# GpSimd waits for the group two in front before it issues a group of gathers, from layer 1 on

## The reference

```python
for l in range(5):
    msg = norm[:, None] * (h[row] + edge_fea)
    agg = segment_sum(msg, col, num_segments=n)
    h = relu(concat([h, agg], axis=1) @ mlp_w[l] + mlp_b[l])
    h = batch_norm(h)            # and relu, but for the last layer
# then: shared expert + two routed experts of eight for each node, added to x
```

## Time and profile before

| | us |
|---|---|
| median of 3 runs | 6880.44 |
| lowest and highest of them | 6827.38, 6889.59 |
| the profiled execution, its own time | 6810.47 |
| span of its instructions | 6808.8 |
| layers 1 to 4 in it (1918 to 5460) | 3542 |

### The profile page before, as it was taken

The page is one execution under the profiler, slowest core; times in us unless marked ns, Lnnn a source line. Parts: engine busy times, 40 slices in busy tenths (PEclk is TensorE's granted clock), DMA queues, the critical chain, the costliest instruction groups (busy, mean ns, idle before and its releaser), DMA issues. The chain is left out here.

```text
span 6808.8 us, 114607 instructions
## 1 busy us (share of the span) xinstructions
PE 5077.8 (75%) x28957; PEld 3394.9 (50%) x28958; DVE 2045.5 (30%) x4409; ACT 1070.7 (16%) x2670; POOL 3252.0 (48%) x3312
## 2 busy tenths in 40 slices
PE   1333377777778878688887788876887869999998
PEld 0222355555544444444444444444444448888876
DVE  7734433333432222322224222232222252000012
ACT  1523300000120000200002000021000032222221
POOL 2888854444455555455554555545555505000014
PEclk9985588988889989898898898988898989999998
DMA  7045144444455555555555555545555531111113
GB/s 264 0 68 158 37 135 135 139 131 127 112 172 167 160 153 163 150 161 160 151 163 147 160 159 164 155 134 172 159 160 154 154 96 69 45 57 59 49 48 92
DMA packets 448168, 874.86 MB, mean 128 GB/s; under 512 B 115986, under 2 KB 261272, under 8 KB 445002
## 3 DMA queue, kind: packets, MB, share of 16 engines
q0 software_dynamic: 184544, 526.38, 27.8%
q10 hardware_dynamic: 97068, 178.12, 9.1%
q1 hardware_dynamic: 166334, 167.82, 8.1%
HBM read 725.48 MB, written 146.57 MB: 128 GB/s over the span
## 5 line engine op out<-in xcount | busy, mean ns | idle before, releaser
L1246 POOL DMA_INDIRECT sets<-rows,index x2480 | 2353.3, 949 | 1974.9 <-issue 714.4
L1938 PE MATMUL bank<-resid,arena 128*128 128x512 bf16 x4116 | 1461.8, 398 | 81.1 <-issue 78.0
L1939 PE MATMUL bank<-sets,arena 128*128 128x256 bf16 x4116 | 1163.2, 283 | 54.2 <-issue 53.4
L1867 PE MATMUL bank<-sets,row_out 128*128 x2432 | 893.8, 403 | 337.3 <-issue 271.4
L1868 PE MATMUL bank<-sets,row_out 128*128 x2432 | 697.7, 287 | 115.7 <-issue 114.2
L1938 PEld LDWEIGHTS bank<-resid,arena 128*128 128x128 bf16 x4116 | 419.4, 102 | 631.9 <-issue 232.9
L2277 PE MATMUL bank<-sets,arena 128*128 128x256 f32 x2480 | 630.2, 387 | 53.5 <-issue 22.5
L461 POOL DMA_INDIRECT dense<-sets x399 | 511.2, 1281 | 224.0 <-issue 106.2
L1276 ACT ACTIVATE index<-arena x620 | 127.3, 205 | 3050.6 <-issue 1605.5
L1867 PEld LDWEIGHTS bank<-sets,row_out 128*128 x2432 | 245.1, 101 | 657.3 <-issue 453.0
L2277 PEld LDWEIGHTS bank<-sets,arena 128*128 128x128 f32 x2480 | 479.3, 194 | 129.8 <-issue 27.4
(11 more groups left out here) (400 smaller groups left out, 5781.8 us busy)
## 6 DMA issues: line engine op xcount, KB each, us to landing
arena<-dense ACTq DMA_DIRECT2D x315, 384.0 KB
arena<-dense ACTq DMA_DIRECT2D x105, 416.0 KB
sets<-rows,index POOLq DMA_INDIRECT x2480
dense<-arena SPq DMA_DIRECT2D x21, 1568.0 KB, 20.9
expert_in<-zero SPq DMA_DIRECT2D x14, 1024.0 KB
expert_out<-zero SPq DMA_DIRECT2D x14, 1024.0 KB
rows<-resid SPq DMA_DIRECT2D x36, 384.0 KB, 2.7
arena<-expert_in SPq DMA_DIRECT2D x54, 256.0 KB, 2.7
```

Of the source, the lines that this page charges most:

```text
L1246: pool.indirect_dma_start(got0_words[:, j, 0:W0 // 2] if first else got[:, j, :], None, rows0 if first else rows, bass.IndirectOffsetOnAxi ...
L1867: pe.matmul(to[:, 0:2 * D], ones, rows_here[:, a:a + 2 * D], start=start, stop=False)
L1938: pe.matmul(bank[:, 5, 0:2 * D], cells, high_parts[:, s, :], start=t == 0, stop=False)
L1939: mm = pe.matmul(bank[:, 5, D:2 * D], cells, low_parts[:, s, :], start=False, stop=False)
```

## The change

In layers 1 to 4 GpSimd makes one more wait before it issues group g: `landed >= g + 3`. As the counter starts at 4, this says that SP has seen g-1 groups, that is, groups 0 to g-2, with their rows in SBUF and their one-hots made. `gated` adds one to a counter that nothing waits for. Layer 0 and everything behind the layers stay as they are, and so do the number of instructions on all other engines, all transfers and their sizes.

```diff
                             if not first:
                                 pool.wait_ge(group_done, now * R + (r + 1))
                                 gated(pool)
+                                pool.wait_ge(landed, now * R + (r + 3))
+                                gated(pool)
                             for j in range(r * K, r * K + K):
                                 pool.indirect_dma_start(
```

## The result

The changed kernel takes 6974.13 us (median, 6954.97 to 7004.72) against 6854.84 us of the kernel before beside it (6827.38 to 6889.59): a ratio of 1.0187, 95% interval 1.0141 to 1.0232. That is 119 us more; forecast were 49. The time lies inside the range of 6840 to 7040, and it is slower by over 1%, to which the prediction had given 0.35, less than the 0.50 of "within 1%".

What follows compares the result with a forecast made beforehand. PE was taken to set the pace, busy 2810 of 3542 us in layers 1 to 4 but not always fed. Stalls of 39 us plus 10 for the clock, 49, added to the median 6880.4 gave 6930 us, range 6840 to 7040.

Steps and rivals of the forecast that it cites:

- Who is held: GpSimd before its gathers: late one-hots of g-2 hold 169 of 488 groups, 609 us together.
- Rows never late: Gathers in layers 1 to 4: rows of g-2 land in time, so waiting for landing alone delays nothing.
- The stalls, 39 us: PE in layers 1 to 4: 25 or so stalls from late groups, most under 2 us, taken as 39 us.
- The worked case, group 179: PE at group 179: issue held to about 2285.6, usable at 2293.1, wanted at 2291.17, 1.9 us of stall.
- The mark of the prediction: Sign of being right: PE's waits at L1867 for L1187 grow from 64.8 us by some 40.
- The clock, 10 us: PE's granted clock: added idle costs 19 us at most, none if the clock is low already; taken as 10.
- Slow stepping, 0 with +20 on one side: PE's long steps without a wait, 163 us in layers 1 to 4: unchanged, or an eighth more, +20 us.
- The dense loads, 0: Dense loads behind ACT's indices: at least 10.9 us from issue to use covers the delay, so no cost.
- third mark: Sign of being wrong: dense matmuls (L1938) begin to wait; none waited for a DMA in the profile before.
- (1) Covered: Rival: all delays vanish in PE's lead, 0 to 15 us, 6885 us; chance 0.20.
- (2) Lockstep: Rival: DVE, gathers and PE hand stalls on; a fourth of 609 us reaches PE, 172 us, 7050; chance 0.22.
- (3) The gentler pace pays: Rival: GpSimd's pauses cut slow steps and late dense loads, -104 us, 6776 us; chance 0.18.

Runs made afterwards that it cites:

- landing only: Kernel before plus a GpSimd wait for the rows of group g-2 alone, not its one-hots: 6893.36 us, 1.0021 of the kernel before.
- the pair with a pause: Kernel before and changed kernel, each with a 0.92 us GpSimd memset behind every group's four gathers: 6769.41 us (0.9872) and 6855.25 us (0.9986).
- Short rows: Kernel before with gathers from layer 1 on fetching 512 bytes a row instead of 1536, sums wrong: 6798.19 us, 1.0041.
- the profiled pair: One profiled execution each of the kernel before (6810 us) and the changed kernel (6959.48 us).
- paused pairs: Kernel before with a 0.52 us GpSimd memset behind every second gather: 6695.89 us, 0.9852; in the last four runs 6043.16 us, 1.0566.
- the paced pair with it: With slow stepping: kernel before and changed kernel, each with a 0.92 us memset behind every group, 6769.41 and 6855.25 us.
- the paced pair without: Without slow stepping: kernel before and changed kernel, each with a 0.52 us memset behind every second gather, 6043.16 and 6036.13 us.
- double pause: Kernel before with two 0.92 us GpSimd memsets behind every group: 6901.05 us, 1.0174.
- the last runs: Four kernels with pauses of several forms, one also with the wait, under a condition where the kernel before took 5692.34 us: 5891.41 to 6155.82 us.

## Why the prediction was right or wrong

**Who is held.** Right. 170 groups were issued before `landed` of g-2 in the trace of before (169 by one-hots in the prediction), none after. The 0.8 us from one-hots to issue stands too: 109 groups are issued 0.8 to 0.9 us after `landed` of g-2. "About 170 cases" ended by L1187 were 134 in the view of waits. Their 637.7 us are GpSimd's whole idle time before them and not the delay that was worked out as 609, so that the two are alike proves nothing.

**Rows never late.** Right: landing only 1.0021 (0.9986 to 1.0057).

**The stalls, 39 us.** The mechanism was right, the term too small: PE's idle time before late groups rose from 34 to 109 us, by 75 (62 against landing only, 70 in the pair with a pause). Directly before held groups stand some 57 us; 14 of these stalls come at four places of the layer (groups 38, 55, 90 and 106 of 124), about 4 us each. In number the forecast was good, 25 or so stalls against 28 late groups more; their size was not. It had most of them under 2 us, 1.7 on average for the 43 us, and measured is 2.7. The worked case, group 179, is one: 3.69 us measured, 1.9 forecast, issue 0.9 us after the one-hots. The other 18 us or so are groups that follow a held one. The mark of the prediction, waits at L1867 for L1187 growing by 40, was badly chosen: that row went from 64.8 to 75.6 us only, because the profile puts most of these stalls under "issue", as it does the 3.69 us above.

**The clock, 10 us.** The term that was off by the largest factor, four to five. The excess of short steps went from 179 to 228 us: 49, and 40 against landing only, 40 in the pair with a pause. The bound of 19 us was made of the ratio of the time at half clock to the idle time. What it missed: the change makes 28 more late groups (10 before, 38 after), each an idle stretch of some us on PE, and with them the stretches at the lower clock rise from 79 to 125, from 683 to 843 us together. An average share per us of idle can't tell which idle brings the clock down; that it is these stretches is suggested by the two counts, not shown. Landing only speaks for caution: with little more idle time before late groups than before (47 us against 34) it has 97 such stretches, 799 us, and still an excess of only 188 us. What the change adds is lower clock while matmuls run.

**Slow stepping, 0 with +20 on one side.** Undersized from the start. I had counted the 296 steps of 0.7 us, 163 us; all steps over 0.6 us, those of 1.4 and 2.1 us in the earlier trace rows included, are 457 us in the same trace. An eighth more of that is 57, not 20. What the change adds to it isn't settled: 128 us against the profiled execution of before, 37 against landing only, -39 in the pair with a pause. One trace of each kernel can't tell. Wrong too was that gathers at place nine or later of a run rise from 256 to 392: with steps of under 1.4 us taken as one run, there are 265 in the trace of before and 228 in that of after.

**The dense loads, 0.** Nearly right: waits for them grew from 25 to 33 us. The prediction's third mark (dense matmuls begin to wait) was met by name, 131 to 242 us in front of them, but these "issue" waits were slow stepping, not loads. For the same reason the rule of the Trainium skill weighed there, "DMA: Bandwidth & Descriptors", section "Issuing engines are not separate DMA queues", gave nothing: its 131 us were no cost of shared DMA engines in this kernel. Short rows halved the traffic and gained nothing.

**The sum.** With the measured terms, 75 for the stalls, 49 for the clock, 8 for dense loads less 34 of turns and 60 of other waits (these two partly the same time, waited for elsewhere), and 128 of slow steps, it is 166 on the profiled pair; against landing only 62 + 40 + 9 + 37 - 68 + 11 = 91. The medians say 119, between the two. The forecast of 49 had the mechanism, but 119 lies outside its own 20 to 90 us, and 6974 just above its 6900 to 6970. That the time lies within 6840 to 7040 is owed to the room left there for lockstep. And by luck 6930 looks nearer to 6974 than it is: the 49 us were added to 6880, where the kernel before took 6855 beside the changed one.

**The rivals.** (1) Covered: refuted where slow stepping is, by 1.0187 and the pair with a pause. Without slow stepping, at least with paced gathers, the wait costs nothing that can be measured, but there hardly a group is held, so that nothing has to be covered. (2) Lockstep: its sum, 172 us, is close to the 169 of the profiled pair, but not by its mechanism: of the 609 us of holding 62 to 75 reach PE as late groups, about a tenth, not a quarter. Its mark, layer 1 over 865 us, was passed at 885, and told little: landing only, which costs next to nothing, took 852 there and 863 and 864 in layers 2 and 4. (3) The gentler pace pays: not with this wait. But the pace itself does where slow stepping is: pauses that are blind to DVE gained 1.3 and 1.5%.

**What lay under it.** The prediction took the late one-hots as the kernel's own rhythm. The paused pairs speak for another account: one-hots are late because PE, and with it DVE's `take`, falls behind in slow stepping. 67 groups of that kernel are issued before `landed` of g-2 with it, 2 without. So the change's price hangs on a condition of the machine: 1.3% in the paced pair with it, 0.1% (-0.4 to 0.6) in the paced pair without. The two pairs have pauses of another form (0.92 us once a group, 0.52 us twice), though nearly the same pace, 5.8 us a group. Open stays what the wait costs without slow stepping and without pauses, where no run was made, and what brings the condition about.

## What to carry to other kernels

Here a producer's wait for the group two in front cost by the worst groups, not by the mean lead: walk the few places where the consumer's helper (here DVE's `take`) runs late, carry the delay on, and add what the clock loses with these idle stretches, here two thirds as much again. "Issue" waits in front of several engines at once are no waits for data; before tuning by them find out whether they are there in every run, as a pause that gained 1.5% with them lost 5.7% without. And a baseline of one profiled execution needs a second: the trace of before (a quick one) and that of landing only (a slow one) give 169 and 94 us for a price of 119.

## What the runs showed of the hardware

Slow stepping: the engines (PE, its weight loads, DVE, ACT and SP) take one instruction per 0.71 us for a while, without a wait. In layers 1 to 4 of the trace of before 228 steps from one weight load to the next are 0.70 to 0.73 us long and 5 are 0.74 to 0.77; on DVE these are 128 and 7, on SP 107 and 4. In the trace of before its share of PE's time outside waits is 4% or less during the first five gathers of a run without a pause, some 10, 20 and 50% during the sixth to eighth, 65 to 85% during the ninth to eleventh, 90% or more from the thirteenth on, and it ends some 2 us after the run. The paused pairs, a gather every 1.25 us and then 0.5 us of rest, still have it (PE's and then GpSimd's order of time):

```profile
2004.66 0.38 PE L1877 MATMUL bank<-sets,row_out 128*128 x1 [0.29 <-issue]
2006.07 0.37 PE L1878 MATMUL bank<-sets,row_out 128*128 x1 [1.03 <-issue]
2006.78 0.59 PE L1877 MATMUL bank<-sets,row_out 128*128 x1 [0.34 <-issue]
...
2004.24 0.94 POOL L1248 DMA_INDIRECT sets<-rows,index  x1 [0.30 <-issue]
2005.18 0.52 POOL L1255 MEMSET idle<- 128x480 f32 x1
2005.86 0.95 POOL L1248 DMA_INDIRECT sets<-rows,index  x1 [0.16 <-issue]
```

It doesn't follow the gathers' bytes (501 us with short rows), is gone at 6.8 us a group (double pause), and is wholly absent from one set of runs, 40 gathers 1.25 us apart included, in which the same kernel took 5692 us instead of 6772 to 6880. Layer 0, which no kernel here changed, took 1002 us in the paused pairs with it and 726 without. That something piles up with each gather and drains between them would fit: at 5.8 us a group, 1.45 us a gather, some slow stepping is left, at 6.8 us, 1.7 us a gather, none. It is argued, not shown, and what piles up, and why not in the last runs, no run shows.
